# A gated recurrent block and two MLPs on one core: the second chunk's mixing moved ahead of the first period, and ScalarE in GpSimd's place for one copy

## What is computed

```
t   = rmsnorm(x, norm1_w)
xb  = causal_depthwise_conv(t @ Wx, conv_w, conv_b)          # 4 taps
r, i = sigmoid(xb @ Wa), sigmoid(xb @ Wi)
a   = exp(-8 * softplus(lam) * r)
b   = sqrt(max(1 - a*a, 1e-12)) * (i * xb)
h   = scan: h[t] = a[t] * h[t-1] + b[t]                      # along the sequence
h1  = x + (h * gelu(t @ Wy)) @ Wo
u   = rmsnorm(h1, norm2_w)
x1  = layernorm(x + h1 + (gelu(u @ Wg) * (u @ Wu)) @ Wd)     # Wg, Wu 256x1024, Wd 1024x256
out = layernorm(x1 + relu(x1 @ W1 + b1) @ W2 + b2)           # W1 256x1024, W2 1024x256
```

## Time and profile before

| | |
|---|---|
| median of 3 runs | 655.78 us (655.57 to 657.83) |
| the profiled execution | 657.96 us |
| its span, first to last instruction | 656.2 us |
| TensorE busy | 613.7 us, 94% of the span |
| VectorE, ScalarE, GpSimd busy | 382.8, 300.9, 214.8 us |
| mean granted clock of TensorE | 0.977 of full speed |

### The profile page before, as it was taken

One profiled execution on the slowest core, in us unless ns is written; L12 is line 12 of the kernel. 1 busy time (PEld: TensorE's weight loads), 2 busy tenths in 40 slices (PEclk: granted clock), 3 DMA queues, 4 the chain that ended last, 5 costly groups with the idle time before them and its releaser, 6 DMA issues.

```text
span 656.2 us, 9445 instructions
## 1 busy us (share of the span) xinstructions
PE 613.7 (94%) x3643; PEld 544.6 (83%) x3643; DVE 382.8 (58%) x689; ACT 300.9 (46%) x555; POOL 214.8 (33%) x313
## 2 busy tenths in 40 slices
PE   8967995989999999999999999999999999999994
PEld 7865884768888888888898889888888888888884
DVE  3853754573648584584648483684657484552544
ACT  5862362326445374436344374447344463323341
POOL 4014203440174224441264125340364124320211
PEclk9977998889999999999999999999999999999999
DMA  8500000100010000000010000001000000000001
GB/s 289 184 1 32 1 1 0 33 0 1 2 33 0 1 33 1 33 1 33 1 32 1 1 33 0 33 1 33 0 2 1 27 7 0 1 33 1 1 32 33
DMA packets 13069, 15.69 MB, mean 24 GB/s; under 512 B 584, under 2 KB 12256, under 8 KB 13024
## 3 DMA queue, kind: packets, MB, share of 16 engines
q1 hardware_dynamic: 13024, 15.09, 6.8%
HBM read 10.89 MB, written 4.19 MB: 23 GB/s over the span
## 4 chain that ended last, share of the span: by engine, by line
PE 72%; DVE 13%; ACT 8%; issue 5%; POOL 2%; DMA 1%; POOLq 0%; ACTq 0%; DVEq 0%
PE psum L272 15%; PE psum L274 14%; PE psum L273 14%; PE psum L280 9%; PE psum L282 8%; PE psum L281 8%; PE psum L287 3%; DVE xv L715 2%; DVE tT_lo L730 2%; DVE gy L724 2%; ACT L529 1%; DVE xb L683 1%; ACT L541 1%; DVE gu_lo L782 1%; ACT decay L529 1%
## 5 line engine op out<-in xcount | busy, mean ns | idle before, releaser
L998 POOL TENSOR_SCALAR gu_hi<-gu_raw 128x512 fp32r<-128x512 f32 x64 | 51.5, 804 | 291.5 <-DVE gu_raw L777 285.1
L573 ACT ACTIVATE hid_raw<-psum,vecs 128x512 f32<-128x512 f32 x64 | 44.0, 687 | 135.6 <-PE psum L274 135.6
L777 DVE TENSOR_TENSOR gu_raw<-psum,gu_raw 128x512 f32<-128x512 f32 x64 | 44.1, 690 | 97.6 <-PE psum L274 93.7
L787 DVE TENSOR_TENSOR hid_lo<-hid_raw,hid_hi 128x512 fp32r<-128x512 f32 x64 | 45.3, 708 | 93.9 <-ACT hid_hi L577 93.9
L564 ACT ACTIVATE gu_raw<-psum 128x512 f32<-128x512 f32 x64 | 38.2, 597 | 92.8 <-PE psum L274 92.1
L280 PE MATMUL psum<-w_hi,hid_hi 128*128 128x256 f32 x256 | 71.7, 280 | 1.2 <-DVE hid_lo L787 0.7
L280 PE MATMUL psum<-w_d_hi,gu_hi 128*128 128x256 f32 x256 | 72.6, 283 | 0.0
L282 PE MATMUL psum<-w_hi,hid_lo 128*128 128x256 f32 x256 | 71.8, 281 | 0.0
L282 PE MATMUL psum<-w_d_hi,gu_lo 128*128 128x256 f32 x256 | 71.8, 281 | 0.0
L281 PE MATMUL psum<-w_lo,hid_hi 128*128 128x256 f32 x256 | 71.7, 280 | 0.0
L281 PE MATMUL psum<-w_d_lo,gu_hi 128*128 128x256 f32 x256 | 71.7, 280 | 0.0
(11 more groups left out here) (143 smaller groups left out, 1558.2 us busy)
## 6 DMA issues: line engine op xcount, KB each, us to landing
xs<-in_L_attn_x_dram SPq DMA_DIRECT2D x8, 512.0 KB, 3.4
out_dram<-row SPq DMA_DIRECT2D x16, 256.0 KB, 2.2
raw<-in_L_ffn_W_dram SPq DMA_DIRECT2D x2, 1024.0 KB, 10.9
raw_gud<-in_L_attn_Wg_dram SPq DMA_DIRECT2D x1, 1024.0 KB, 7.5
raw_gud<-in_L_attn_Wu_dram SPq DMA_DIRECT2D x1, 1024.0 KB, 9.6
raw_gud<-in_L_attn_Wd_dram SPq DMA_DIRECT2D x1, 1024.0 KB, 11.9
raw_xyai<-in_L_attn_Wx_dram SPq DMA_DIRECT2D x1, 256.0 KB, 2.6
raw_xyai<-in_L_attn_Wy_dram SPq DMA_DIRECT2D x1, 256.0 KB, 2.9
```

Source lines behind the costliest of these rows:

```text
L573: nc.scalar.activation(hid_raw[:, w % SLOTS, :], bank[:, :], ACT.Relu, bias=vec("b1", m)).then_inc(relu_ready, 1)
L777: nc.vector.tensor_tensor(gu_raw[:, r % SLOTS, :], psum[UP][:, :], gu_raw[:, r % SLOTS, :], ALU.mult).then_inc(gu_ready, 1)
L787: nc.vector.tensor_tensor(hid_lo[:, w % SLOTS, :], hid_raw[:, w % SLOTS, :], hid_hi[:, w % SLOTS, :].bitcast(FP32), ALU.subtract).then_inc ...
L998: nc.gpsimd.tensor_scalar(gu_hi[:, r % SLOTS, :], gu_raw[:, r % SLOTS, :], 1.0, 0.0, ALU.mult, ALU.add).then_inc(gu_hi_ready, 1)
```

## The change

Chunk 1 is mixed earlier. Its transposes, its x, y, a and i projections, convolution and tanh move from rounds 0 to 5 into the prologue, in among chunk 0's mixing; its exp, square and square root, its scan, its out projection and its h1 stay in period 0, at rounds 0 to 6 (out projection and h1 in rounds 5 and 6, where they were in round 7). For that:
- x of chunk 1 is loaded right behind Wi.
- The high halves of the weights y, a, i, u, d, 1 and 2 are made by GpSimd, not by ScalarE (g was already GpSimd's); those of 1 and 2 only in rounds 0 to 3. VectorE's low halves of u are cut in two around chunk 0's scan, those of 1 and 2 into single pieces in rounds 1, 2, 4 and 5.
- Fillers: 14, 36 and 16 become 9, 28 and 18.
- In the first eight rounds gate and up products take turns between two banks each, since SECOND is still free, and TensorE's waits for gelu and gu_raw reach one round further back.

In all periods `hy_hi` moves from GpSimd to ScalarE, its target from tT to mT, and `hy_lo` stands ahead of `gate_lo` in round 5.

The diff, cut to its core:

```diff
-            for n in ("x", "y", "a", "i", "g", "u", "o", "d"):
+            for n in ("x", "y", "a", "i"):
                 load_w(n)
             load_x(1)
-            load_w("1")
+            for n in ("g", "u", "o", "d", "1"):
+                load_w(n)
...
+                if r == 1:
+                    pe.wait_ge(tanh_a_ready, 4)
+                elif r >= 2:
+                    pe.wait_ge(gelu_ready, r - 1 if r < KH else r)
+                product(gate_bank(r)[:, :], "g", m, uT_hi, uT_lo).then_inc(gate_done, 1)
...
             split_done("y")
             mix_y(0, bank=DOWN)
-            keep_running(14)
+            transpose_t(1)
+            keep_running(9, SECOND)
             split_done("a", "i")
-            mix_decay(0)
             pe.wait_ge(vecs_ready, 1)
-            mix_input(0, bank=GATE)
-            keep_running(36)
+            mix_decay(0, bank=GATE)
+            mix_input(0, bank=SECOND)
+            mix_x(1)
+            pe.wait_ge(gy_ready, KD)
+            mix_y(1, bank=DOWN)
+            pe.wait_ge(tanh_a_ready, KD)
+            keep_running(28, GATE)
             split_done("o")
-            mix_out(0)
-            keep_running(16)
+            mix_out(0, bank=GATE)
+            pe.wait_ge(tanh_i_ready, KD)
+            keep_running(18, SECOND)
             transpose_u(0)
+            mix_decay(1, bank=SECOND)
+            pe.wait_ge(gy_ready, 2 * KD)
+            mix_input(1, bank=DOWN)
             split_done("g", "u")
...
+            def hy_hi(c):
+                for m in range(KD):
+                    act.wait_ge(hy_ready, 2 * c + m + 1)
+                    nc.scalar.activation(mT_hi[:, m, :], gy[:, m, :], ACT.Copy).then_inc(hy_hi_ready, 1)
...
+            def first_period(r):
+                n = 1
+                if r == 1:
+                    room(n)
+                if r == 3:
+                    scan_both(n)
+                if r == 6:
+                    for q in range(PAIRS):
+                        add_mix(n, q)
+                gate_times_up(r)
+                if r == 0:
+                    gated_input(n)
+                if r == 4:
+                    gated(n)
+                    hy_lo(n)
+                gate_lo(r)
+                if r == 0:
+                    weight_lo("d")
...
-            def hy_hi(c):
-                for m in range(KD):
-                    pool.wait_ge(hy_ready, 2 * c + m + 1)
-                    nc.gpsimd.tensor_scalar(tT_hi[:, m, :], gy[:, m, :], 1.0, 0.0, ALU.mult,
-                                            ALU.add).then_inc(hy_hi_ready, 1)
```

More of the change, by code:

```diff
@@ L427, in round_of @@
                     down(r - 1)
-                if mixing and m == 3:
+                if mixing and m == 3 and p >= 1:
                     mix_input(n)
@@ L596, in round_of @@
                 mixing = n < CHUNKS
-                if mixing and m == 1:
+                if mixing and m == 1 and p >= 1:
                     conv_start(n, 1)
@@ L802, in units, with scan_both @@
                 return 0 <= r < UNITS
+            def scan_both(c):
+                for k in range(KD):
+                    scan_input(c, k)
+                for k in range(KD):
+                    scan(c, k)
+            def first_period(r):
[14 more added lines that the diff above has]
+                gate_lo(r)
+                if r == 0:
+                    weight_lo("d")
+                if r == 1:
+                    weight_lo("1", ks=[0])
+                if r == 2:
+                    weight_lo("1", ks=[1])
+                if r == 4:
+                    weight_lo("2", ks=[0])
+                if r == 5:
+                    weight_lo("2", ks=[1])
+                if r == 7:
+                    split_lo(uT_lo, uT_hi, uT_hi_ready, uT_lo_ready, n)
             def round_of(r):
@@ L817, in round_of @@
                     normalise(s, 1, 1, out_ready)
-                if m == 5 and mixing and p >= 1:
-                    for k in range(KD):
-                        scan_input(n, k)
-                    for k in range(KD):
-                        scan(n, k)
-                if m == 6 and mixing and p >= 1:
-                    add_mix(n)
+                if m == 5 and mixing:
+                    scan_both(n)
+                if m == 6 and mixing:
+                    for q in range(PAIRS):
+                        add_mix(n, q)
                 if units(r):
@@ L913, in _ @@
             room(0)
-            weight_lo("u", "n2")
             gated_input(0)
-            for m in range(KD):
-                scan_input(0, m)
-            for m in range(KD):
-                scan(0, m)
+            weight_lo("u", "n2", ks=[0])
+            scan_both(0)
             gated(0)
             hy_lo(0)
-            add_mix(0)
+            weight_lo("u", "n2", ks=[1])
+            convolve_half(1, 0, 0)
+            add_mix(0, 0, bank=GATE)
+            convolve_half(1, 0, 1)
+            add_mix(0, 1, bank=GATE)
+            convolve(1, 1)
+            convolve(1, 2)
+            xb_lo(1)
             split_lo(uT_lo, uT_hi, uT_hi_ready, uT_lo_ready, 0)
-            for r in range(CHUNKS * KH + 2 * KH + 5):
+            for r in range(KH):
+                first_period(r)
+            for r in range(KH, UNITS + 2 * KH + 5):
                 round_of(r)
@@ L999, in gate_hi, with weight_hi @@
                                         ALU.add).then_inc(gu_hi_ready, 1)
+            def weight_hi(n, norm=None, ks=None):
+                pool.wait_ge(w_loaded[n], DMA)
+                for k in range(pieces[n]) if ks is None else ks:
+                    nc.gpsimd.tensor_scalar(piece(flat(w_hi[n]), n, k), piece(raw_of[n], n, k),
+                                            vec(norm, k) if norm else 1.0, 0.0,
+                                            ALU.mult, ALU.add).then_inc(hi_split[n], 1)
             def round_of(r):
@@ L1004, in round_of @@
                 mixing, first, second = n < CHUNKS, 0 <= f < CHUNKS, 0 <= s < CHUNKS
-                if mixing:
+                if mixing and p >= 1:
                     if m == 0:
@@ L1030, in round_of @@
                         add_x_h1(n)
-            def weight_hi(n, norm):
-                pool.wait_ge(w_loaded[n], DMA)
-                for k in range(pieces[n]):
-                    nc.gpsimd.tensor_scalar(piece(flat(w_hi[n]), n, k), piece(raw_of[n], n, k), vec(norm, k), 0.0,
-                                            ALU.mult, ALU.add).then_inc(hi_split[n], 1)
             nc.gpsimd.memset(ident[:, :], 0.0).then_inc(ident_zero, 1)
```

205 lines of the change are left out of this document (108 added, 97 removed).

## The result

The changed kernel takes 639.87 us, the median of four runs (638.95 to 639.99), against 656.38 us for the kernel before beside it (655.57 to 657.83): ratio 0.9748, 95% interval 0.9725 to 0.9771. It is faster by 2.5%. The forecast was 626.3 with a range up to 634: the sign is right, the size is not, and the time lies outside the range. The profiled execution took 639.91 us, its span 638.0 instead of 656.2.

A forecast was written before the change was run, and what follows sets the result against it. TensorE, 94% busy, was taken as the bound, with time to gain in the first period and six recurring waits. Terms +1.3 - 23.4 - 1.4 - 6.0 = -29.5 us off the median 655.78 gave 626.3 us, range 622 to 630 (8 in 10: 621 to 634).

The forecast's parts named there:

- The bound: TensorE, busy for 94% of the span; only its idle and slow time, in two places, can be saved.
- C: Second period's first gate product to mix_x(2), 6.95 us before: -1.4 us, bounds 0 to -1.5.
- D: Out projections of later periods: ScalarE copying the high half ends the wait, six times 1.0: -6.0 us (-3 to -6.1).
- the six waits: TensorE's waits for tT_lo behind 160 us, about 1.0 us in each later period, 6.1 us in all.
- Rival 2: ScalarE's copies do not close the waits in later periods: 629 to 632 us, chance 0.08.
- the price of a meeting of VectorE and GpSimd: Where both engines run together, operations take a third more: a tap 1.04 us instead of 0.79.
- the rest fits into the 2.8 between: Prologue, lambda steps ahead of ScalarE's exp: of about 2 us added or slowed, only 0.6 reach the exp.
- Term A: Up to the first gate product: worked to 54.7, plus 0.6 for meetings, 55.3 us; +1.3, bounds +0.3 and +4.5.
- Term B: First period, 64.0 us before: 35.3 work, 4.1 waits, 1.2 clock, 40.6 us; -23.4, bounds -24.6 and -18.
- Rival 1: VectorE and GpSimd stand still for each other, before chunk 0's scan and in the first period: 632.5 us, chance 0.17.
- Rival 3: TensorE's clock falls to 1.2 GHz in the first period and stays down: 657.7 us, not faster, chance 0.02.
- The signs: Wrong if GpSimd pieces exceed 2 us and VectorE lags over 4 us, or clock under 0.9, in the first period.

The follow-up runs named there:

- experiments 9 and 10: Kernel before with only hy's high half moved to ScalarE, low half earlier: 650.96 us; changed kernel with this undone in the later periods: 647.55 us.
- experiment 7: Changed kernel with 9 more fillers ahead of chunk 0's out projection and 9 more ahead of the transposes of u: 636.27 us.
- the best kernel: Changed kernel with W1, W2, Wd high halves on ScalarE, w_d_lo early, lambda steps split, GpSimd starting big weights after chunk 0's xb_lo: 626.50 us.
- experiment 3: Changed kernel with the high halves of W1 and W2 made by ScalarE in rounds 1 and 3 instead of by GpSimd: 636.50 us.
- experiment 6: Changed kernel with fillers in TensorE's two longest gaps of the first period, 14 in round 1 and 9 in round 4: 636.64 us.
- experiment 1: Changed kernel with GpSimd starting on the big weights only when VectorE's lambda steps are done: 643.55 us.

## Why the prediction was wrong

- **The bound, and terms C and D: right.** The first period and the six waits were where time could be had, C gave 1.5 us and D 6.3 in the five whole periods. Undone alone D costs its 6 us and done alone it gains them (experiments 9 and 10). Rival 2 did not come.
- **The step that failed: the price of a meeting of VectorE and GpSimd.** The prediction took a third on top (1.04 instead of 0.79 us) from the earlier trace rows, two long operations of nearly one length, where "a third more" and "until the other ends" can't be told apart. With it, it said that of the lambda steps "the rest fits into the 2.8 between". They took 6.1 us for 2.9; with the low half of xb, 2.21 for 1.36, they put exp at 29.81 instead of about 27.4: 2.3 us on the out projection, 1.7 by the lambda steps and the rest by xb. In the first period the same price made w_d_lo and gu_lo later, 2.8 us of idle time. The rule of the Trainium skill, page "SBUF — State Buffer", section "Who interferes with whom", that the later one is blocked until the first has finished, was quoted and given its price; the runs agree with it (0.16 us at rest, 0.85 to 1.00 behind pieces of 1024 columns, 0.65 behind 512).
- **The trace of before could have told.** The prediction divided merged rows: 4.76 / 6 = 0.79 us for a tap, 3.20 / 2 = 1.6 for a piece. Taken singly they are uneven (the first piece and the first tap):

```profile
12.78 2.10 POOL L1035 TENSOR_SCALAR w_g_hi<-raw_gud,vecs 128x1024 fp32r<-128x1024 f32 x1 [3.42 <-DMA raw_gud<-in_L_attn_Wg_dram]
...
15.19 1.33 DVE L683 SCALAR_TENSOR_TENSOR xb<-xv,vecs,xb 128x512 f32<-128x512 f32 x1 [1.22 <-ACT xb L503]
```

  The next tap took 0.75 us and the next piece 1.12. So each mean had a held operation in it.
- **Term A, +5.5 for +1.3.** From the working's 54.7: 2.3 for the late exp; about 1.5 for the out projection at a clock of 0.53, which the prediction had as a bound (the fillers of experiment 7 gave 1.6 back); and 0.9 between the out projection and the first gate product, where the working had 14.9 us and the best kernel, at full clock, takes 15.8. That makes 59.4. The 0.9 lies where GpSimd's rms and normalising of chunk 0 stand beside chunk 1's taps, 4.2 us instead of 3.1. That these meetings cost it was read in the trace only; no run takes them away.
- **Term B, -15.6 for -23.4.** The order of the waits was right, each was larger: w_d_lo 3.5 for 2.4, gu_lo 2.4 for 0.7, normed 1.3 for 0.6, uT_lo 1.7 for 0.4, together 4.8 us. The first two are for the most part GpSimd's pieces of W1 and W2 (experiment 3); normed and uT_lo still take 2.7 us of idle time between them there and in the best kernel, so they are mostly too tight a working. The lower clock took 3.0 us for 1.2, since two gaps brought it and not one (experiment 6), and the work was 36.6 us for 35.3.
- **The 12 us in one sum:** 2.3 and 2.8 for the holds, 1.5 and 1.8 for the clock behind the gaps, 2.0 for normed and uT_lo, 1.3 for the work and 0.9 in the prologue, less the 0.6 that term A had added for meetings: 12.0.
- **Rival 1 was what happened**, given a chance of 0.17 and 632.5 us. Its mechanism was right. Its time was 7 us short, since it priced the holds without the lower clock behind the gaps that they open, and kept the sum's other terms. Rival 3 named the clock but only as all or nothing; it took 1.5 us at one place and 3.0 at two.
- **The signs did not warn.** The first gate product and the period lay outside what was named, but the signs of being wrong stayed quiet: the longest wait was 3.5 us, where more than 4 was the sign, and the clock in the period 0.93, where it was under 0.9.

## What to carry to other kernels

Before giving GpSimd work, list every VectorE operation that it will run beside, the tiny ones above all, and charge each with the rest of GpSimd's running operation, and GpSimd with the rest of VectorE's. A chain of small dependent steps on the path is the worst place for that. Take the duration of an operation from single rows: a mean over merged rows can have a held one in it. When a new wait of about 2 us or more for TensorE appears in a plan (1.9 to 3.5 us here), price it twice, once as idle time and once with the work behind it at the lower clock, and try a few fillers there. When two versions differ by 2 us, compare the clock behind the gaps that both have before the edit is given the credit.

## What the runs showed of the hardware that I had not expected

- The same gap is followed by either clock. All kernels with the new order wait 3.27 us for gu_raw in the second period. The 10 us behind it in the kernel after:

```profile
127.92:132.92 5.00, 4.06 (x10) 3.21 (x11) 3.01 (x5) 1.12 (x2) 0.99 (x1) 0.50 0.00 0
132.92:137.92 5.00, 5.00 (x21) 4.06 (x20) 2.00 (x3) 1.34 (x3) 0.62 (x1) 0.86 0.00 0
```

and in that with the lambda steps first:

```profile
126.74:131.74 5.00, 4.01 (x17) 3.05 (x18) 3.67 (x6) 1.86 (x3) 0.99 (x1) 1.00 0.00 0
131.74:136.74 5.00, 5.00 (x29) 4.38 (x28) 1.38 (x2) 1.20 (x2) 0.62 (x1) 1.00 0.00 0
```

  0.50 or 1.00, 10 matmuls or 17 begun in the same stretch, and 53.88 - 51.64 = 2.2 us in the end. Shorter gaps did the same: the 2.04 us before 42.13 were followed by 0.53 and the 2.28 before 53.05, in the same execution, by 1.00; 2.27 us at those transposes were followed by 0.57 in experiment 3 and by 1.00 in the best kernel. With halved pieces it was the other way round than in the changed kernel: 2.52 us before the out projection were followed by 1.00 and 2.27 before the transposes by 0.50. What decides, the runs don't show.
- Executions of one kernel differ in this too. The kernel before with hy on ScalarE took 648.67, 649.11, 652.81 and 652.91 us, at mean clocks of 0.975 for the first two and 0.967 for the others; the profiled one is 652.81. So a median of four could move by 2 us without any edit.
- Seven steps of 2 columns beside half-size pieces took 3.83 us, where they take 1.34 at rest: a small operation is held as a large one is.
- Operations with one SBUF input were held too: the tensor_scalar of 2 columns, 0.99 us for 0.16, and the two on xv in experiment 1, 2.44 us for 0.76. The reciprocal, with one input too, was not: 0.17 us beside a piece of 1024 columns.
